# Cross-attention on one core: the row of maxima sent from ScalarE's queue, the loads of residuals from SyncE's

## The reference

```python
q = _split_heads(hidden_states @ Wq.T, H)          # x: (2, 2048, 640)
k = _split_heads(text @ Wk.T, H)                   # text: (2, 77, 1024)
v = _split_heads(text @ Wv.T, H)
scores = jnp.einsum('bhsd,bhld->bhsl', q, k) * sm_scale
probs = jax.nn.softmax(scores, axis=-1)
out = _merge_heads(jnp.einsum('bhsl,bhld->bhsd', probs, v)) @ Wo.T + bo
return out + hidden_states                         # the residual
```

## Time and profile before

| | before |
|---|---|
| median of 3 runs | 430.57 us (430.57 to 431.01) |
| the profiled execution | 431.85 us, of which the profile's span is 430.0 us |
| TensorE busy | 418.5 us (97%) |
| ScalarE, VectorE, GpSimd busy | 307.9, 266.8 and 305.7 us |
| mean granted clock of TensorE | 0.992 of full speed |

### The profile page before, as it was taken

One profiled execution on the slowest core, in us unless ns is written; L12 is line 12 of the kernel. 1 busy time (PEld: TensorE's weight loads), 2 busy tenths in 40 slices (PEclk: granted clock), 3 DMA queues, 4 the chain that ended last, 5 costly groups with the idle time before them and its releaser, 6 DMA issues.

```text
span 430.0 us, 8447 instructions
## 1 busy us (share of the span) xinstructions
PE 418.5 (97%) x2550; PEld 227.5 (53%) x2550; DVE 266.8 (62%) x555; ACT 307.9 (72%) x594; POOL 305.7 (71%) x268
## 2 busy tenths in 40 slices
PE   8999996999999999999999999999999999999996
PEld 6977764566665444444444444444444444444442
DVE  0354785657788666775577666756577655565733
ACT  1737985778889997779668895789667975966720
POOL 8437796698999789496749695587659594664560
PEclk9999999799999999999999999999999999999999
DMA  8997549135865537343554338333763347345203
GB/s 279 366 334 265 201 135 319 48 122 186 283 224 179 165 128 255 129 148 124 198 206 169 141 123 270 126 123 134 235 217 126 127 147 244 124 156 194 95 24 123
DMA packets 41779, 77.32 MB, mean 180 GB/s; under 512 B 5264, under 2 KB 6416, under 8 KB 41744
## 3 DMA queue, kind: packets, MB, share of 16 engines
q1 hardware_dynamic: 30944, 57.21, 38.1%
q10 hardware_dynamic: 10800, 19.67, 14.1%
HBM read 33.40 MB, written 10.49 MB: 102 GB/s over the span
## 4 chain that ended last, share of the span: by engine, by line
PE 90%; ACT 3%; DVE 2%; DMA 2%; issue 2%; POOL 0%; DVEq 0%; ACTq 0%
PE ps_q L921 28%; PE ps_o L921 26%; PE ps_s L986 10%; PE ps_pv L993 7%; PE ps_m L972 5%; PE ps_den L998 4%; PE ps_o L890 2%; DMA q_packed<-mxT 2%; ACT x_f L513 1%; PE ps_m L1043 1%; PE ps_s L877 1%; PE ps_m L977 1%; PE ps_q L869 1%; PE ps_q L1043 1%; PE ps_s L1043 1%
## 5 line engine op out<-in xcount | busy, mean ns | idle before, releaser
L445 POOL TENSOR_TENSOR p_lo<-p_f,p_hi 77x512 f16<-77x512 f32 x160 | 182.9, 1164 | 91.4 <-ACT p_hi L580 90.1
L576 ACT ACTIVATE p_f<-ps_s 77x512 f32<-77x512 f32 x160 | 94.4, 590 | 22.2 <-PE ps_s L986 21.1
L921 PE MATMUL ps_o<-attn,wo 128*128 128x512 f16 x435 | 108.7, 380 | 0.5 <-DVE sums L781 0.3
L921 PE MATMUL ps_q<-x,wq 128*128 128x512 f16 x450 | 102.1, 379 | 0.0
L580 ACT ACTIVATE p_hi<-ps_s 77x512 f16<-77x512 f32 x160 | 93.7, 585 | 4.1 <-PE ps_den L998 4.0
L712 DVE TENSOR_REDUCE mx<-ps_m 128x4 f32<-128x308 f32 x160 | 69.3, 475 | 42.0 <-PE ps_m L972 41.2
L921 PEld LDWEIGHTS ps_q<-x,wq 128*128 128x128 f16 x450 | 43.8, 98 | 53.2 <-issue 0.8
L986 PE MATMUL ps_s<-q_packed,k_packed 128*77 128x512 f32 x160 | 65.1, 450 | 3.5 <-DMA q_packed<-mxT 3.3
L921 PEld LDWEIGHTS ps_o<-attn,wo 128*128 128x128 f16 x435 | 37.8, 98 | 45.7 <-issue 7.5
L701 DVE SCALAR_TENSOR_TENSOR q_lo<-ps_q,q_scale,q_hi 128x512 fp32r<-128x512 f32 x30 | 22.5, 751 | 58.6 <-ACT q_hi L559 58.5
L559 ACT ACTIVATE q_hi<-ps_q,q_scale 128x512 fp32r<-128x512 f32 x30 | 20.5, 682 | 37.0 <-PE ps_q L921 36.9
(11 more groups left out here) (125 smaller groups left out, 593.9 us busy)
## 6 DMA issues: line engine op xcount, KB each, us to landing
q_packed<-q_hi SPq DMA_DIRECT2D x80, 256.0 KB, 2.5
x_f<-in_x SPq DMA_DIRECT2D x45, 256.0 KB, 4.3
q_packed<-q_lo SPq DMA_DIRECT2D x40, 256.0 KB, 3.2
x_res<-in_x ACTq DMA_DIRECT2D x35, 256.0 KB, 2.8
out<-x_res ACTq DMA_DIRECT2D x35, 256.0 KB, 2.7
wq_sb<-in_wq SPq DMA_DIRECT2D x10, 320.0 KB, 4.2
wo_sb<-in_wo SPq DMA_DIRECT2D x10, 320.0 KB, 4.0
wk_sb<-in_wk SPq DMA_DIRECT2D x8, 320.0 KB, 5.5
```

The costliest lines, as they stand in the source:

```text
L445: nc.gpsimd.tensor_tensor(p_lo[:, i, :], p_f[:, i, :], p_hi[:, i, :], ALU.subtract).then_inc(plo_done, 1)
L576: nc.scalar.activation(p_f[:, i, :], ps_s[i % 2][0:L, :], ACT.Exp, scale=SCALE).then_inc(pf_done, 1)
L921: last = nc.tensor.matmul(ps[:, :], w[:, k, P * c:P * (c + 1)], a[:, c, :], start=(c == 0 and n == 0), stop=(c == G - 1 and n == 2))
```

## The change

The 8 KB transfer of the maxima is issued by ScalarE, right behind the copy that makes them, and no longer by SyncE. The 256 KB loads of residuals are issued by SyncE, at the place where the maxima were sent, and no longer by ScalarE. Which bytes move, and what each consumer waits for, stays the same. ScalarE now waits for its own copy to be complete before it issues the transfer.

```diff
-            def load_max(t, g):
-                sp.wait_ge(mT_copied, nth(t, g) + 1)
-                sp.dma_start(q_packed[0:1, g % RS, :, :].bitcast(F32).rearrange("o i (a c) -> o (i a) c", c=P),
-                             mxT[:, g % RS, :].bitcast(F32)).then_inc(pack_in[g % RS], 16)
+            def load_residual(t, k):
+                if is_last(t):
+                    return
+                if exists(slot_before(t, k)[0]):
+                    sp.wait_ge(out_in[k % RS], 16 * slot_uses(*slot_before(t, k)))
+                sp.dma_start(x_res[:, k % RS, :], x[t, :, k, :]).then_inc(res_in[k % RS], 16)
...
                 load_w_again(wq_sb, wq, wq_in, q_chunks, 1, wq_again_at(t, g))
                 load_w_again(wo_sb, wo, wo_in, o_chunks, 0, wo_again_at(t, g))
-                if exists(shift(t, g, 1)[0]):
-                    load_max(*shift(t, g, 1))
+                for tile in out_tiles(*shift(t, g, 1)):
+                    load_residual(*tile)
...
-            def load_residual(t, k):
-                if is_last(t):
-                    return
-                if exists(slot_before(t, k)[0]):
-                    act.wait_ge(out_in[k % RS], 16 * slot_uses(*slot_before(t, k)))
-                act.dma_start(x_res[:, k % RS, :], x[t, :, k, :]).then_inc(res_in[k % RS], 16)
+            def send_max(t, g):
+                act.wait_ge(mT_copied, nth(t, g) + 1)
+                act.dma_start(q_packed[0:1, g % RS, :, :].bitcast(F32).rearrange("o i (a c) -> o (i a) c", c=P),
+                              mxT[:, g % RS, :].bitcast(F32)).then_inc(pack_in[g % RS], 16)
...
                 if exists(shift(t, g, 1)[0]):
                     copy_max(*shift(t, g, 1))
+                if exists(shift(t, g, 1)[0]):
+                    send_max(*shift(t, g, 1))
...
                 attn_high(at, [c for c in (2, 3) if c in chunks])
-                for tile in out_tiles(*shift(t, g, 1)):
-                    load_residual(*tile)
                 attn_high(at, [c for c in (4,) if c in chunks])
```

## The result

| | before | changed |
|---|---|---|
| median, the two run side by side | 430.79 us (430.57 to 431.68, 4 runs) | 440.78 us (438.72 to 442.11, 4 runs) |
| ratio, with its 95% interval | | 1.0197 [1.0161, 1.0233] |
| profiled execution, and its span | 431.85 us, 430.0 us | 442.11 us, 440.3 us |
| TensorE busy | 418.5 us | 423.2 us |
| mean granted clock | 0.992 | 0.988 |

The changed kernel is 2.0% slower by the ratio (1.6 to 2.3%) and 10.0 us slower by the medians, whose quotient is 1.023. The forecast was 427.0 us with a range up to 430.6, so it was wrong, and on the wrong side of no change.

What follows compares the result with a forecast made beforehand. PE bounds the kernel, with gains only at start-up in its 3.3 us wait for maxima and the low clock behind it. Gain 5.1 less cost 1.5 is 3.6: 430.57 - 3.6 = 427.0 us, range 425.8 to 430.6.

Steps and rivals of the forecast that it cites:

- What bounds the kernel: Whole kernel: PE is busy 97% of the span; gains lie at start-up, in its 3.3 us wait for the maxima.
- The gain of 5.1 us in step 5: Step 5, last reduction of maxima: 2.5 us from scores starting earlier plus 2.6 us from the clock staying high.
- the first: Step 4's send of maxima: alone on ScalarE's queue, it lands in 2.3 us instead of 5.0.
- Rival 2: Step 4's send: it shares the backlog, takes 5.0 us again and the clock falls; 432.3 us, chance 0.13.
- The second reason: SyncE in step 3: not held by the send, it issues loads of x earlier; packings move up some 0.8 us.
- The cost of 1.5 us on ScalarE: ScalarE's delay reaching PE in steps 3, 6, 11 and 12: 1.5 us together, 1.3 to 2.0 by issue price.
- Its size: ScalarE behind each copy: delay of about 0.6 us per step, 0.38 of it issue; 0.75 with a dearer issue.
- Its reach: Delay reaches PE only in steps 3 (0.25 us), 6 and 11 (0.6 each), 12 (0.3); nothing in five-scaling steps.
- The clock: PE's short waits, 0.4 and 0.7 us elsewhere, left the clock high, so it was taken to stay at 2.4 GHz.
- Rival 3: ScalarE: the send costs 1.2 us per step instead of 0.6; 430.6 us, no change, chance 0.08.
- Earlier loads: SyncE at start-up: loads issued sooner counted only as gain, with 0.4 us for other loads at the range's fast end.
- The residuals: SyncE loading residuals ahead of its packing, with more than 5 us of cover: costs nothing.

Runs made afterwards that it cites:

- experiment 4: The changed kernel, send still right behind the copy, with SyncE outside the tile loop waiting for the copy where it used to send; 437.29 us, 1.0104.
- experiment 10: The changed kernel with sends two activations later and SyncE waiting for copies outside the tile loop, but SyncE sends steps -1 to 3; 431.94 us, 0.9983.
- experiment 11: The kernel before, with only step 3's send issued by ScalarE, two activations behind the copy, and SyncE waiting for that copy; 429.44 us, 0.9929.
- experiment 12: The kernel before, with only step 3's send issued by ScalarE, two activations behind the copy, and SyncE not waiting for it; 428.22 us, 0.9898.
- experiment 3: The changed kernel with the send two activations later and, outside the tile loop, SyncE waiting for the copy where it used to send; 428.66 us, 0.9931.
- experiment 1: The kernel before, with only the residual loads moved to SyncE, behind its send of the maxima; 432.36 us, 0.9997.
- experiment 9: The changed kernel with the send right behind the copy only in the loop over tiles 3 to 5, two activations later elsewhere; 431.54 us, 0.9983.
- experiment 8: The kernel before, with SyncE's reloads of weights moved behind its send of the maxima; 435.69 us, 1.0061.

## Why the prediction was wrong, point by point

**What bounds the kernel** was read rightly: PE, and at start-up the one wait of 3.3 us with the low clock behind it.

**The gain of 5.1 us in step 5** was there: 4.6 us by the table of copies, with the clock at 1.00. About 1.0 us of it went again in step 6, where the clock fell (1.35 us lost; 0.33 in experiment 4, where it didn't). Of its two reasons the first was wrong. I had the send land in 2.3 us because it is alone on its queue; on such a queue, behind an unchanged backlog, it took 5.0 (experiment 10), and in the changed kernel itself 5.2 in step 0. The statement of the Trainium skill that I had weighed against it (Trainium Kernel Development and Optimization, "Key Constraints": another engine's queue saves only the issue) agrees with these runs. That the engines take turns between queues (DMA: Bandwidth & Descriptors, "Queues, rings and completion order") gave the 32 packets no head start that was worth anything here. Rival 2 had the queue right, at a chance of 0.13; its price of 5.0 us didn't fall due because the backlog was older by then: the last packing was issued 4.1 us ahead of the send (68.34 and 72.45 us), and not 2.3 (66.27 and 68.54).

The second reason, that SyncE's backlog starts earlier when it doesn't stand at step 3's send, carries part of the gain (experiments 11 and 12). The other part I had no term for: step 3's send now lands later beside the loads, PE waits in step 4, and so step 4's send goes out later too. The last packing before it is issued 0.3 to 0.8 us earlier than before (65.44 to 65.93 us in experiments 3, 11 and 12, against 66.27), and the send itself 1.1 to 2.8 us later (69.60 to 71.31, against 68.54). So the wait isn't taken away as I had it: it goes from 3.3 us at one place to 1.9 to 2.4 us in all in these three, at one place or two, and the clock stays up or falls for less. In the changed kernel itself the steps up to 4 run 3.0 us later than before, and steps 4 and 5 wait 1.05 and 1.02 us.

**The cost of 1.5 us on ScalarE** is the term on which the sign turned. Three things in it were wrong.
- Its size: 0.6 us per step, of which 0.38 was the issue, scaled from SyncE's. The issue took 0.51 to 0.55 us in most steps. One number in the scaling was wrong: 2.48 / 5 = 0.50 us for a tile of x is the pace of five loads in one place, and not what an issue takes, which is 0.34 us in the median of the run before (the view of that line; minimum, median and maximum in ns):

```profile
L354 SPq DMA_DIRECT2D x_f<-in_x x45: 327/342/1059, 7.4 to 355.9; - x45
```

  With it the estimate would have been 0.57 x 0.33 / 0.34 = 0.55 us. The delay was 0.74 to 0.76 us at start-up (0.90 to 0.92 less 0.16), 0.82 to 0.91 in most steps of the loop.
- Its reach: I tested the slack only against PE's `max_scores`. The path over `q_lo` and the sums on VectorE was not looked at, and steps 8 to 11 lost 0.4 to 0.7 us each where I had put nothing; step 7, which has the wait behind step 6, lost 2.3 with the clock. Step 3 lost 0.76 us, where I had 0.25. In the five-scaling steps "the delay fits in, just" was too close to call by my own dearer price, 0.75 us against 0.65; it came to 0.91, and some 0.6 us was lost per tile.
- The clock: I had it that short waits don't move it. But those that the delay makes are not short: 1.16 us behind step 6 and 1.50 us at 153.5 us, on top of the 0.4 and 0.72 us that were there. The clock fell behind both, and in steps 7 and 12, where it did, 2.30 and 2.18 us were lost (0.70 in step 7 of experiment 4, without a fall). I had priced that at nothing.

Rival 3 was this mechanism, but with a chance of 0.08, and it ended at no change because it left out the clock and VectorE's path. The stand alone costs 7.5 us (experiment 4 against 3), not 1.5: this is the term that failed.

**Earlier loads,** which I had only as a gain, cost 4.0 us in the presence of that stand (the changed kernel against experiment 4), some 2 of them by the clock; without it they cost 1 us or nothing that can be told. No term of mine had them, and the DMA share over 30 to 40 us, 0.80 before, showed that there was little room.

**The residuals** cost nothing that can be told, as predicted (experiment 1).

**What adds up, and what doesn't.** Of the 10.3 us of span, PE's listed waits are 4.9 (3.9 for `q_hi`, 1.1 for the sums, -0.1 for the maxima). The clock's share is 1.9, by the reckoning of experiment 4: 5.3 for 0.988, less 3.4 for 0.992. 0.9 us is there before the first send. The other 2.6 us I can't place in the rows; part may be that busy times of matmuls are modelled at their ends.

**Left open:** why the clock fell behind a wait of 1.16 us in step 7 and behind three short ones in step 6, and not behind waits of 1.16, 1.18 and 1.21 us in experiments 3 and 12 or one of 1.95 us in step 1 of experiment 9; and what lowers it in some executions of a kernel and not in others (experiments 3 and 8).

## What to carry to other kernels

Put a transfer that waits for its own engine's result one or two instructions behind the place where it becomes ready: it goes out at the same moment and the sequencer doesn't stand (here 10.5 us of 430, the clock's part included). When an engine is delayed at every step, test the delay against every path out of the first late result, at the dear end of the price, and count the waits that exist already: added to them it may be long enough to lower the clock. Another engine's queue doesn't carry a transfer past a backlog; look instead at when the backlog is issued, and how much of it is still to land when the transfer goes out.

## What I had not expected of the hardware

- A transfer of 8 KB, alone on ScalarE's queue, took 5.0 us with six of SyncE's transfers still to land (experiment 10), 2.6 with three (experiment 3), and 1.8 at the least.
- ScalarE's issue of the 8 KB took 0.51 to 0.65 us and its issue of 256 KB 0.33 to 0.45 us (0.35 in the median): the size in bytes doesn't decide it.
- A wait and an issue that stand behind two activations in the list, which the sequencer has passed on by then, cost nothing; the same two ahead of them cost 0.74 us or more each time.
- The granted clock fell behind single waits of PE of 1.16 and 1.50 us in a stretch otherwise busy, and not behind others as long; it fell once behind waits of 0.60 us and less, and it differs between executions of one kernel.
